# Expert rows scattered into fixed rooms and results accumulated in DRAM, in place of gathered tiles and a combine by table

## The reference, cut to what matters

```python
def _route(x, gate_w, gate_bias):
    logits = jnp.einsum('nh,eh->ne', x, gate_w)
    scores = jax.nn.sigmoid(logits)
    sb = scores + gate_bias                      # 16 experts in 4 groups: the best 2 groups stay,
    ...                                          # and of these the best 4 experts: tidx
    w = jnp.take_along_axis(scores, tidx, axis=1)
    w = w / (jnp.sum(w, axis=-1, keepdims=True) + 1e-20)
    return (tidx, w * SCALE)                     # SCALE = 2.5
# each of the 1024 tokens: sum over its 4 experts of w * (silu(x w1) * (x w3)) w2, plus one shared expert
# D = 256 columns, EI = 192 hidden columns of an expert, E = 16 experts, TOPK = 4
```

## Time and profile before

| | us |
|---|---|
| median of 3 runs (1140.32 to 1142.3) | 1140.37 |
| the profiled execution | 1141.2 |
| its span, first to last instruction | 1139.4 |
| last attention block of layer 1 ends (its last product of values) | 920.6 |
| router of both batches done | 949.0 |
| first gate and up product of the tile loop | 987.6 |
| last scatter issued, landed | 1115.3, 1117.9 |

### The profile page before, as it was taken

The page is one execution under the profiler, slowest core; times in us unless marked ns, Lnnn a source line. Parts: engine busy times, 40 slices in busy tenths (PEclk is TensorE's granted clock), DMA queues, the critical chain, the costliest instruction groups (busy, mean ns, idle before and its releaser), DMA issues. The chain is left out here.

```text
span 1139.4 us, 18929 instructions
## 1 busy us (share of the span) xinstructions
PE 995.2 (87%) x6572; PEld 875.3 (77%) x6572; DVE 827.9 (73%) x1594; ACT 710.7 (62%) x1377; POOL 424.0 (37%) x442
## 2 busy tenths in 40 slices
PE   1789979898899989999999999999999978588981
PEld 1668878688688768898888889898888867487870
DVE  6687765777623379788888888788888966774645
ACT  3477756776633468777777777777787833074550
POOL 5164432543167700402003020402006463767771
PEclk9899989999999999999999999999999999699996
DMA  4100000000311200000100001000001323253335
GB/s 132 33 1 1 1 5 1 1 1 14 103 42 35 68 1 1 1 1 2 38 1 1 1 1 38 1 1 1 14 16 41 95 70 88 60 168 101 104 103 203
DMA packets 41437, 45.38 MB, mean 40 GB/s; under 512 B 15040, under 2 KB 35648, under 8 KB 40832
## 3 DMA queue, kind: packets, MB, share of 16 engines
q1 hardware_dynamic: 36832, 31.84, 9.2%
q0 software_dynamic: 4512, 12.33, 3.6%
HBM read 35.89 MB, written 8.26 MB: 39 GB/s over the span
## 5 line engine op out<-in xcount | busy, mean ns | idle before, releaser
L331 PE MATMUL PS<-R 128*128 128x512 f32 (+3 forms) x2669 | 574.8, 359 | 40.2 <-POOL R L539 7.9
L331 PEld LDWEIGHTS PS<-R 128*128 128x128 f32 x2669 | 427.9, 194 | 98.7 <-issue 22.5
L1641 DVE TENSOR_TENSOR R<-PS,R 128x512 fp32r<-128x512 f32 x320 | 205.1, 682 | 37.6 <-ACT R L1314 36.6
L1314 ACT ACTIVATE R<-PS 128x512 fp32r<-128x512 f32 x320 | 174.6, 596 | 79.1 <-PE PS L773 78.0
L1277 ACT ACTIVATE FA<-PS,nmax 128x1024 f32<-128x1024 f32 (+1 forms) x160 | 192.6, 1204 | 35.6 <-DVE nmax L1630 18.9
L786 PE MATMUL PS<-R 128*128 128x256 f32 x1408 | 202.6, 289 | 10.5 <-DVE FB L1649 9.1
L773 PE MATMUL PS<-eye,FA 128*128 128x128 f32 x1408 | 185.3, 276 | 13.4 <-DVE R L1641 5.2
L773 PEld LDWEIGHTS PS<-eye,FA 128*128 128x128 f32 x1408 | 160.8, 141 | 46.0 <-issue 21.3
L786 PEld LDWEIGHTS PS<-R 128*128 128x128 f32 x1408 | 178.8, 190 | 18.7 <-issue 14.5
L1630 DVE TENSOR_REDUCE nmax<-PS 128x1 f32<-128x1024 f32 x128 | 155.5, 1220 | 33.9 <-PE PS L331 23.4
L497 POOL TENSOR_SCALAR R<-R 64x512 fp32r<-64x512 f32 x40 | 25.8, 645 | 320.2 <-ACT R L1429 260.0
(11 more groups left out here) (234 smaller groups left out, 1241.6 us busy)
## 6 DMA issues: line engine op xcount, KB each, us to landing
wst<-w_in SPq DMA_DIRECT2D x4, 1024.0 KB, 4.9
wst<-we_in SPq DMA_DIRECT2D x16, 256.0 KB
wst<-we_in SPq DMA_DIRECT2D x24, 128.0 KB
FB<-k_in SPq DMA_DIRECT2D x16, 128.0 KB, 2.0
FA<-parts SPq DMA_DIRECT2D x4, 512.0 KB, 4.9
wst<-w_in SPq DMA_DIRECT2D x3, 512.0 KB, 7.2
x<-x_in SPq DMA_DIRECT2D x2, 512.0 KB, 6.2
FB<-ctxT_in SPq DMA_DIRECT2D x2, 512.0 KB, 4.4
```

Of the source, the lines that this page charges most:

```text
L331: last = mm(out, a, b, start=(n == 0), stop=(n == len(passes) - 1), skip_group_check=skip)
L1314: a_(L.pt[0][:, (u // 2) % 2, 4 * g_:4 * g_ + 4, (u % 2) * P:(u % 2) * P + P], L.turn(u, g_).rearrange("p (t n) -> p t n", t=4), ACT.Copy) ...
L1641: inc(v.tensor_tensor(lo, turned, hi.bitcast(F32), ALU.subtract), "p_lo")
```

## The change

The gathers, the token table and the combine are replaced.

- In DRAM, `rows` becomes 16 rooms of 1024 rows, one room for each expert, and 128 rows more. A row has 273 words: 256 columns of the token, 16 scores (zero where the expert is not among its four), and the token's number. SP fills all of `rows` (18.0 MB) and two result tensors `sums` of 1152 x 256 (2.4 MB together) from one zeroed row in SBUF, early in layer 1; the last word of a filled row is the number of a spare row.
- When a token's rank within its expert is known, its place is the expert's room plus the rank. POOL scatters the rows there: for every 128 tokens four indirect DMAs, 32 in all, in two chunks of 16 (`place_rows(0)` for batch 0, `place_rows(1)` for batch 1).
- The routing of batch 0 (norm, turn, `router(0)`, sigmoid, `choose(0)`) moves into the units of the last attention block; `choose(1)` runs after the norm of batch 1, without jobs between its steps. The one-hot matrices, the token table and the two lists are gone.
- A tile is now 128 consecutive rows of a room. SP loads it by a plain DMA at an address from a register (`places`), into one of eight buffers (`HELD`), the ninth and later ones after the scatter of the tile eight before has landed.
- ACT weights a tile's result when it copies it to `put` (the weight of each row comes from `tile_share` on DVE), and POOL scatters it with an added sum (`compute_op=ALU.add`) into `sums0` or `sums1` by turns. Since the sums are read and written, the scatter of tile j waits until that of tile j - 2 has landed.
- At the end SP reads 2 MB (eight DMAs of 256 KB), DVE adds the two sums (four instructions of 128 x 512) and adds them to `x` with each token's factor (eight of 128 x 256).
- The split of the experts' weights is shared out anew: POOL alone for 0 to 2, ACT high and POOL low for 3 to 10, ACT and DVE for 11 to 15. SP's loads of experts 9 to 15 are written between its tile loads.

```diff
+ROOM = NB * S
+ROW = D + E + 1
+HELD = 8
+PLANES = 2
+CHUNKS = ((0, 4), (4, 4))
+SPLIT_POOL = 11
+HI_AT = {1: 9, 2: 10, 4: 11, 6: 12, 8: 13, 10: 14, 12: 15}
+LO_AT = {5: 11, 7: 12, 9: 13, 11: 14, 13: 15}
+LOAD_AT = {3: (9, 10), 7: (11, 12), 9: (13,), 11: (14,), 13: (15,)}
...
+        sp.wait_ge(s["preset"], 1)
+        every = rows_d.rearrange("(c p) n -> p c n", p=P)
+        for c in range(0, E * ROOM // P + 1, 43):
+            sp.dma_start(every[:, c:c + 43, :], fill.unsqueeze(1).to_broadcast([P, 43, ROW])).then_inc(s["filled"], 16)
...
+        for c, (t0, n) in enumerate(CHUNKS):
+            sp.wait_ge(s[f"placed_rows{c}"], 64 * n)
+        sp.wait_ge(s["places_set"], 1)
...
+            if j >= HELD:
+                sp.wait_ge(s[f"sent{j % PLANES}"], 16 * ((j - HELD) // PLANES + 1))
+            sp.dma_start(got[:, j % HELD, :], rows_d[bass.ds(at[j % 4], P), :]).then_inc(s[f"got{j % HELD}"], 16)
+            for e in LOAD_AT.get(j, ()):
+                next_expert(e)
...
+        def place_rows(c):
+            t0, n = CHUNKS[c]
+            pool.wait_ge(s["slots_set"], c + 1)
+            for t in range(t0, t0 + n):
+                for k in range(4):
+                    i = 4 * t + k
+                    g.indirect_dma_start(rows_d, bass.IndirectOffsetOnAxis(ap=slots[:, i:i + 1], axis=0), row_tiles[t],
+                                         None).then_inc(s[f"placed_rows{c}"], 16)
...
-        for j in range(RINGS, TILES + 7):
-            if j < TILES:
-                gather(j)
-            if j >= 7:
-                scatter(j - 7)
+            if j >= PLANES:
+                pool.wait_ge(s[f"sent{plane}"], 16 * (j // PLANES))
+            g.indirect_dma_start(sums_d[plane],
+                                 bass.IndirectOffsetOnAxis(ap=got[:, j % HELD, ROW - 1:ROW].bitcast(U32), axis=0),
+                                 put[:, j % RINGS, :], None, compute_op=ALU.add).then_inc(s[f"sent{plane}"], 16)
...
+            a_(put[:, j % RINGS, :], PS[:, 6 + j % 2, 0:256], ACT.Copy, scale=tile_weight[:, j:j + 1]).then_inc(s["y_out"], 1)
...
+                elif u == 16:
+                    choose(0)
...
+        for w in range(4):
+            dve.wait_ge(s[f"back_in{w}"], 16 * PLANES)
+            for i in range(1, PLANES):
+                do(v.tensor_tensor(back[0][w], back[0][w], back[i][w], ALU.add))
+            for t in (2 * w, 2 * w + 1):
+                inc(v.scalar_tensor_tensor(x[:, t, :], back[0][w][:, D * (t % 2):D * (t % 2) + D], inverse[:, t:t + 1],
+                                           x[:, t, :], ALU.mult, ALU.add), "out_ready")
```

More of the change, by code:

```diff
@@ new lines, in _ @@
+        pool.wait_ge(s["o_sum"], BLOCKS * (2 * NG1 + 2))
+        row_numbers(4, 4)
+        pool.wait_ge(s["at_lo"], 4 + 4 * NG1)
+        for h in range(2):
+            half = before16[:, 128 * h:128 * h + 128]
+            step(g.iota(half.bitcast(I32), [[1, 8], [-1, E]], base=8 * h, channel_multiplier=0))
+            step.wait()
+            step(g.tensor_scalar(half, half.bitcast(I32), 0.0, float(P), ALU.is_gt, ALU.mult))
+        step.wait()
+        pool.sem_inc(s["consts"], 1)
+        expert_lo(3)
@@ L1063, in fill @@
                     last.then_inc(s["ln_turned" if kt else "ln_half"], 1)
+                if not more and u in (9, 11):
+                    kt = u // 2 - 4
+                    pe.wait_ge(s["ln_xn"], 4 * NB + 1)
+                    if kt == 1:
+                        pe.wait_ge(s["ln_lo"], 6 * NB + 1)
+                    for t in range(TT):
+                        last = nc.tensor.transpose(PS[:, 5, t * P:t * P + P], late0[t][:, kt * P:kt * P + P], eye_ap)
+                    last.then_inc(s["ln_turned" if kt else "ln_half"], 1)
+                if not more and u == 13:
+                    pe.wait_ge(s["gw_split"], 1)
+                    router(0)
                 if more and u == UNITS - 2:
@@ new lines, in find_slots @@
+        def find_slots(c):
+            t0, n = CHUNKS[c]
+            place, slot = bo[:, 0:E * n].rearrange("p (t e) -> p t e", e=E), bo[:, 64:64 + 4 * n]
+            ranks = PS[:, 0 if c else 3, 256:256 + E * n].rearrange("p (t e) -> p t e", e=E)
+            dve.wait_ge(s["ranked"], c + 1)
+            do(v.tensor_tensor(place, ranks, room_at.unsqueeze(1).to_broadcast([P, n, E]), ALU.add))
+            for t in range(n):
+                last = v.tensor_tensor(product[:, 4 * t:4 * t + 4, :], chosen[:, t],
+                                       place[:, t].unsqueeze(1).to_broadcast([P, 4, E]), ALU.mult)
+            do(last)
+            do(v.tensor_reduce(slot, product[:, 0:4 * n, :], AX.X, ALU.add))
+            if c:
+                do(v.tensor_copy(count, PS[:, 0, 256 + E * n:256 + E * n + E]))
+            inc(v.tensor_copy(slots[:, 4 * t0:4 * (t0 + n)], slot), "slots_set")
@@ L2009, in _ @@
[L2009 removed]
+        choose(1)
+        job(1, 1)
+        find_slots(1)
+        job_low(1, 1)
+        job(2, 0)
         job_low(2, 0)
[L2011 to L2013 removed]
         job(3, 1)
         job_low(3, 1)
[L2018 to L2019 removed]
@@ new lines, in _ @@
+        do(v.tensor_tensor(owner, tile_iota.unsqueeze(2).to_broadcast([P, 48, E + 1]),
+                           base.unsqueeze(1).to_broadcast([P, 48, E + 1]), ALU.is_ge))
+        experts, room, part, where = (bo[0:1, 48 * i:48 * i + 48] for i in range(4))
+        ahead = FA[0:1, 0:768].rearrange("p (j e) -> p j e", e=E)
+        do(v.tensor_reduce(experts, owner[0:1, :, 0:E], AX.X, ALU.add))
+        do(v.tensor_tensor(ahead, owner[0:1, :, 0:E], spare[0:1, :].unsqueeze(1).to_broadcast([1, 48, E]), ALU.mult))
```

514 lines of the change are left out of this document (249 added, 265 removed).

## The result

The changed kernel takes 1147.63 us (median of 8 runs) where the kernel before, on the same chip, takes 1142.05: the ratio is 1.0058, 95% interval 1.0041 to 1.0076. It is slower by 0.6%, where faster was forecast. The profiled execution took 1146.89, its span is 1145.1.

What follows compares the result with a forecast made beforehand. POOL's gathers and scatters, 2.57 us a tile, were taken to bound the loop, with a serial tail behind. Start +8.9, loop -21.4, landing +1.4, tail -9.1 make -20.2: span 1139.4 to 1119.2, median 1120, range 1111 to 1147.

Steps and rivals of the forecast that it cites:

- (b): Tile loop: accumulating scatters replace POOL's issue as the bound, making the kernel slower, above 1143 us; chance 0.17.
- (a): Tile loop: POOL or the accumulate still sets the pace, two tiles in 4.7, time 1127 to 1138; chance 0.22.
- (d): Tile loop: PE waits for SP's queued loads or ACT, 2.57 a tile, 1143 us; chance 0.11 together with (c).
- (c): Before the loop: each row scatter costs 2.0 instead of 1.27, giving 1143 us; chance 0.11 together with (d).
- the tail: After the last landing: read-back of 2 MB, additions and store take 12.4 us against 21.5, 9.1 less.
- the fill: Early in layer 1: 20.4 MB of zero stores take 106 us, fit between SP's loads, and cost nothing.
- The landing of the accumulating scatter: Tile loop: 3.9 us from issue to landing, the middle between 2.5 and 5.4; loop end 1.4 us later.
- two tiles need at least one landing plus the 0.30 of issue: 4.2: Tile loop: each scatter waits for the one two tiles older, so 4.2 us for two tiles, 2.1 for one.
- neither bounds nor leaves slack: Tile loop: the scatters' 2.1 us a tile is as much as PE needs.
- PE's path: Tile loop: PE at 2.08 us a tile from 996.5, ending with its last scatter at 1106.9.
- I allow 3 us: First 14 tiles: cost of still splitting experts 9 to 15, with ACT waiting in order for their loads.
- loads now come from SP, up to eight tiles ahead, so they lie ready: Tile loop: tiles' rows are loaded ahead, so POOL issues one DMA a tile, 1.29 us, and PE's 2.08 bounds.

Runs made afterwards that it cites:

- e15: The change with eleven buffers, three sums, low parts of experts 5 to 10 on DVE before the loop, and tile loads ahead of expert loads in SP's queue: 1122.24 us.
- e8: The change with one sum instead of two, so only one accumulating scatter is in flight: 1243.5 us, one run.
- e3: The change with four sums instead of two: 1151.82 us, ratio 1.0083 to the kernel before.
- e10: The change with eleven tile buffers instead of eight and three sums instead of two: 1139.06 us, ratio 0.9979 to the kernel before.
- e13: The change with low parts of experts 5 to 10 on DVE before the loop and weights of 9 to 15 earlier: 1140.66 us.
- e16: e15 with two sums instead of three: 1132.87 us, ratio 0.9904 to the kernel before.
- e4: The change with low parts of experts 9 and 10 moved from POOL to DVE, in the loop: 1147.63 us, ratio 1.0040 to the kernel before.
- e5: The change with weights of experts 11 to 15 loaded and split later (valid for these inputs only): 1151.89 us, ratio 1.0078 to the kernel before.
- e9: The change with eleven tile buffers instead of eight: 1151.12 us, ratio 1.0070 to the kernel before.
- e2: The change with the added sum left out, so a result's scatter overwrites its rows: 1133.91 us, ratio 0.9928 to the kernel before.
- e7: The change with late weights as in e5 and no added sum as in e2: 1136.73 us, ratio 0.9930 to the kernel before.

## Why the prediction was wrong, step by step

The forecast was 1120, and 1147.63 was measured; the span is 25.9 us above the sum's 1119.2. Slower is the outcome of rival (b), but it did not come by (b) alone: two tiles took 4.96 us in the loop, between the 4.7 of (a) and the 5.02 from which (b) decides, and the mechanism of (d) in the first tiles made up the rest.

**Right.** Router 0 on PE took 2.74 us (3.0 forecast), `choose(0)` 6.3 (7), the block's output was there at 933.5 (933.7). POOL's 32 scatters took 1.27 each without a wait and ended at 989.4 (989.2; the sum writes 935.8 and 6.5 where its text has 935.5 and 6.3, half a microsecond too much), so rival (c) was wrong. The first product came at 997.07 (996.5), the first accumulating scatter at 1010.20 (1009), the tail took 13.2 (12.4), the fill nothing. PE's own pace is 2.08: e15 goes at it, and from its first product at 993.92 to the end of the last at 1096.2 it takes 102.3, where 104.6 were worked out. The landing of the accumulating scatter was taken as 3.9, the middle of two far bounds, and is 3.8 in e8, with one in flight, and 3.9 on the median in e3, e10, e13, e15 and e16; no row pointed to the middle, so that is luck.

**Wrong, the chain of two sums.** The step that failed is "two tiles need at least one landing plus the 0.30 of issue: 4.2". The 0.30 belongs to a DMA that waits for nothing. One that waits for a landing starts 0.7 after it (e8, and the chain of waits), and the 19 landings in the change's chain from 1036 on take 3.65 to 4.68, 4.04 on the mean. Two tiles took 4.96 on the mean of tiles 14 to 40. Of the 0.76 above 4.2 the gap is 0.4 and the landing 0.1; the rest is not split further, but in it POOL waits for results, which come late when PE waits for rows (2.44 us at 1065.38). A gap of 0.4 us in a step repeated 23 times, with no slack beside it, is 9 us; "neither bounds nor leaves slack" was the sentence to distrust. By its own terms the chain did not quite meet PE's path either: 23 steps of 4.2 from 1009 and the last landing of 3.9 end at 1109.5, not at the 1107.7 of 47 x 2.1. From tile 15 to the last landing the change took 88.8 us; the forecast's own steps give 74.4 (1032.4 to 1106.8), 14.4 less. POOL's issue of 1.55 against the 0.99 of a plain scatter was not seen either, but does not bind: 1.85 with its gap is less than PE's 2.08.

**Wrong, the first fifteen tiles.** "I allow 3 us" for the weights and "loads now come from SP, up to eight tiles ahead, so they lie ready" failed together. By them tile 15 comes at 996.5 + 1.7 + 15 x 2.08 + 3 = 1032.4; it came at 1043.18. Of these 10.8 us, 0.6 are the later start. The gathers stood in POOL's queue and the weights in SP's; the change puts both into SP's, so a tile's load waits for what an expert's load waits for. PE's three longest waits there have three sources: 2.56 us ACT, in order behind the load of expert 11; 3.34 the buffer of tile 8, held until the late scatter 0 had landed; 2.66 tile 12 behind expert 14 in SP's queue. Behind the last two, the next groups of products add 1.45 and 1.02 us over the usual 1.89. Rival (d) named the queue and ACT, but as a way to lose all of the gain, with a small chance and apart from (b). In fact both happened, one in the first tiles and one in the rest: 0.6 + 10.2 + 14.4, and 0.7 of tail, are the 25.9.

**Why taking one away did nothing.** Scatters free the buffers, buffers hold up loads, loads in one queue hold up each other: behind each bound stood the next, 0.2 us a tile below it (2.48 by the sums, 2.26 by the ring, 2.08 by PE). So three sums in the change gave 0.25% (intervals overlap), the same edit beside early weights, eleven buffers and rows first 0.95% (intervals apart).

What stays open is how the loss of the first tiles in the change divides among late scatter 0, weights and buffers: e4, e5 and e9 each took one away by itself, and none gained time that the intervals can tell. Rows first was not tried with eight buffers, where tile 8 has to wait for scatter 0.

## What to carry to other kernels

When a change replaces one bound by a chain of "issue, land, issue again", price one link from the landing to the next issue, not from a row that waits for nothing, and ask what the slack to the next bound is; where it is under a tenth of a step, forecast the chain. A queue that gets a second kind of load also gets that load's waits: write down, for each entry, what the one ahead of it waits for. And when an edit that removes a shown wait gains nothing, look for the next bound close behind it before dropping the theory.

## What the runs showed of the hardware

**An accumulating scatter.** 128 rows of 1 KB cost POOL 1.55 us to issue (0.97 plain), land after 3.8 to 3.9 (2.4 to 2.5 plain), and fill the DMA engines three times as long. The queue's share of 16 engines in 1045 to 1110 (packets, MB, share), the change with 27 accumulating scatters, then e2 with 31 plain ones:

```profile
q0 software_dynamic: 3777, 3.44, 46.1%
```

```profile
q0 software_dynamic: 1440, 3.93, 16.5%
```

That is about 65 x 0.461 / 27 = 1.11 us of all sixteen engines for one, against 0.35. The packets come out of the pages' totals for this queue: 3792 for the 79 plain scatters of e2 are 48 each, so the change's 8304 are 32 x 48 and 47 x 144, three times as many for an accumulating one. The Trainium skill, "DMA: Bandwidth & Descriptors", section "Rules for kernel authors", says that an accumulating DMA reads its destination and writes it later with nothing held in between, so that another one to the same bytes has to wait for the semaphore; that is the wait measured here, and no run tried to do without it.

**DVE held up by POOL.** The subtraction of 128 x 768 at 991.17 above took 5.20 us beside four low parts of POOL (989.55 to 995.5), and 0.95 in e15, where POOL does nothing of the kind. In e2 a cast of 128 x 16, ahead of that, took 6.19 beside the low parts of experts 5 and 6 (962.96 to 968.95) and moved DVE's later work back; so the low parts of 7 and 8 (990.07 to 996.1) met one of 1 x 48, which took 6.59, and the first product came 4 us later than in the change. In the change the same cast was over at 960.4, before the low parts began. e7 and e9 show the same two rows of 6.19 and 6.59. The row of e15, then the two of e2:

```profile
990.80 0.95 DVE L2170 TENSOR_TENSOR FB<-FB 128x768 f32<-128x768 f32 x1
```

```profile
962.80 6.19 DVE L2034 CAST FB<-bo 128x16 uint32<-128x16 f32 x1
...
989.55 6.59 DVE L2144 TENSOR_TENSOR FB<-bo 1x48 int32<-1x48 f32 x1
```

The Trainium skill, "SBUF — State Buffer", section "Who interferes with whom", says that a DVE instruction with two inputs in SBUF contends with a POOL instruction that reads SBUF, and that the later one is blocked while the other runs. The row at 991.17 agrees: it started 1.6 us after POOL's first low part. The recorded starts of e2's two rows are 0.2 and 0.5 us before POOL's, so there the rows do not show which came first. In all three DVE ended only when all four of POOL's instructions were done.
